# Attention scores from float32r parts on half of TensorE's rows, with maxima and exponentials of two heads side by side

## The reference

```python
q, k, v = proj(wq, bq), proj(wk, bk), proj(wv, bv)      # (4, 16, 1024, 16)
scores = jnp.einsum('bhqd,bhkd->bhqk', q, k) * scale
mask = jnp.triu(jnp.full((t, t), NEG, jnp.float32), k=1)
attn = jax.nn.softmax(scores + mask, axis=-1)
x = _layernorm(x + jnp.einsum('bhqk,bhkd->bhqd', attn, v).transpose(0, 2, 1, 3).reshape(b, t, d) @ wo + bo)
top1 = jnp.argmax(jnp.einsum('bh,he->be', x.mean(axis=1), Wr) + br, axis=-1)
x = _layernorm(x + relu(x @ W1[top1] + b1[top1]) @ W2[top1] + b2[top1])
```

## Time and profile before

| | us |
|---|---|
| median of 3 runs (956.9 to 964.15) | 957.01 |
| the profiled execution | 961.64 |
| its span, first to last instruction | 959.9 |
| PE busy in it | 803.6 (84%) |
| DVE busy | 636.3 (66%) |
| POOL busy | 452.2 (47%) |
| ACT busy | 441.7 (46%) |

### The profile page before, as it was taken

The page is one execution under the profiler, slowest core; times in us unless marked ns, Lnnn a source line. Parts: engine busy times, 40 slices in busy tenths (PEclk is TensorE's granted clock), DMA queues, the critical chain, the costliest instruction groups (busy, mean ns, idle before and its releaser), DMA issues.

```text
span 959.9 us, 16241 instructions
## 1 busy us (share of the span) xinstructions
PE 803.6 (84%) x5232; PEld 472.7 (49%) x5232; DVE 636.3 (66%) x2036; ACT 441.7 (46%) x801; POOL 452.2 (47%) x795
## 2 busy tenths in 40 slices
PE   3678879788988899979998799979998799992596
PEld 2333224224443455647672365647662365582586
DVE  1678768776888676756788677756888473262153
ACT  1005645554546565535445655535445557611231
POOL 6001324435354764544454764544454466664553
PEclk9769989999999999979999999979999799996799
DMA  3823531550525262302353262302343200002100
GB/s 102 102 27 39 101 43 14 101 68 3 68 63 80 66 111 38 44 13 30 50 88 76 57 111 40 41 13 32 49 48 78 85 12 14 13 12 65 40 23 23
DMA packets 44247, 49.99 MB, mean 52 GB/s; under 512 B 14722, under 2 KB 28802, under 8 KB 44162
## 3 DMA queue, kind: packets, MB, share of 16 engines
q1 hardware_dynamic: 44162, 48.95, 30.1%
HBM read 18.64 MB, written 4.19 MB: 24 GB/s over the span
## 4 chain that ended last, share of the span: by engine, by line
PE 58%; DVE 20%; SPq 6%; issue 5%; DMA 5%; POOL 3%; ACT 2%; DVEq 0%; POOLq 0%; ACTq 0%
PE o_ps L401 12%; PE max_ps L372 11%; PE dense_ps L495 9%; PE dense_ps L480 8%; PE exp_ps L385 8%; DVE max_ps L528 6%; PE dense_ps L419 5%; DVE partial_max L531 4%; PE dense_ps L430 3%; DMA stage<-in_w 2%; PE dense_ps L447 2%; DVE part_rest L565 2%; DMA inv_rows<-sums 1%; DVE partial_max L528 1%; DVE ln_in L639 1%
## 5 line engine op out<-in xcount | busy, mean ns | idle before, releaser
L718 ACT ACTIVATE prob<-exp_ps 128x512 f32<-128x512 f32 x576 | 333.1, 598 | 297.0 <-PE exp_ps L385 293.3
L528 DVE CUSTOM_DVE_ANT_0 max_ps<-max_ps,causal 128x512 f32<-128x512 f32 (+3 forms) x512 | 240.1, 512 | 96.5 <-PE max_ps L372 95.8
L372 PE MATMUL max_ps<-stack_k,stack_q 96*128 96x512 bf16 (+3 forms) x768 | 234.7, 349 | 72.2 <-DVE partial_max L528 31.7
L794 POOL TENSOR_SCALAR_AFFINE_SELECT prob<-prob 128x128 f32<-128x128 f32 x512 | 142.6, 299 | 252.3 <-ACT prob L718 250.9
L385 PE MATMUL exp_ps<-stack_q,stack_k 99*128 99x512 bf16 (+3 forms) x768 | 226.2, 337 | 18.9 <-ACT prob L718 15.5
L531 DVE TENSOR_REDUCE partial_max<-max_ps 128x1 f32<-128x512 f32 x256 | 171.3, 684 | 85.4 <-PE max_ps L372 84.8
L372 PEld LDWEIGHTS max_ps<-stack_k,stack_q 96*128 96x128 bf16 x768 | 67.1, 100 | 259.3 <-DVE partial_max L531 83.0
L401 PE MATMUL o_ps<-prob,v_ones 128*32 128x512 f32 (+3 forms) x1536 | 164.4, 517 | 0.0
L480 PE MATMUL dense_ps<-x1T_hi,w_hi 128*128 128x256 f32 x256 | 86.9, 339 | 35.0 <-POOL w_lo L844 21.4
L385 PEld LDWEIGHTS exp_ps<-stack_q,stack_k 99*128 99x128 bf16 x768 | 73.5, 100 | 65.1 <-ACT prob L718 27.1
L859 POOL TENSOR_TENSOR hidden_lo<-stage,hidden_hi 128x512 fp32r<-128x512 f32 x64 | 82.1, 1284 | 48.2 <-DVE hidden_hi L673 48.0
(11 more groups left out here) (73 smaller groups left out, 1016.6 us busy)
## 6 DMA issues: line engine op xcount, KB each, us to landing
stage<-in_w SPq DMA_DIRECT2D x32, 256.0 KB, 2.7
stack_k<-parts SPq DMA_DIRECT2D x64, 96.0 KB, 2.8
stack_q<-parts SPq DMA_DIRECT2D x64, 96.0 KB, 3.2
xT_sb<-in_xT SPq DMA_DIRECT2D x4, 1024.0 KB, 5.4
stack_k<-parts SPq DMA_DIRECT2D x64, 64.0 KB, 3.3
stack_q<-parts SPq DMA_DIRECT2D x64, 64.0 KB, 3.2
x<-in_x SPq DMA_DIRECT2D x4, 1024.0 KB, 6.7
out<-ln_in SPq DMA_DIRECT2D x16, 256.0 KB, 2.2
```

What stands on the lines that cost most here:

```text
L372: mm = TE.matmul(bank[:, at * P:(at + count) * P], stack_q[slot][0:ROWS, c, i * P:(i + 1) * P], stack_k[slot][0:ROWS, c, k0 * P:(k0 + coun ...
L528: op = VE.tensor_tensor_reduce(src, src, causal[:, BANK - count * P:], 1.0, MASKED, ALU.add, ALU.max, dst)
L718: SE.activation(prob[tile % P_RING][:, :], exp_ps[tile % 2][:, :], ACT.Exp, scale=scale).then_inc(s_exp, 1)
L794: GE.affine_select(out=part, in_=part, compare_op=ALU.is_ge, fill=0.0, base=0, pattern=[[1, P]], channel_multiplier=-1).then_inc(s_cut, 1)
```

## The change

Queries and keys are cut into two float32r parts rather than three bf16 ones. A head then needs 48 rows (50 with the maxima), which lie in one half of the array's 128 rows: heads 0 and 2 of a group in the lower, 1 and 3 in the upper. The order of the maxima tiles is such that in each step the maxima tile and the exponentials tile are of different halves. The causal constant is added to the maxima tile by TensorE: two more matmuls for each diagonal block, with a unit matrix, on the half of the tile's own head. So DVE needs one reduction for every tile. TensorE's program is written for two steps at a time: both steps' scores, then the products with the values, then the dense work. The inverses of the sums are spread by DMA rather than by DVE, each head's rows go to `attn` by DMA rather than by POOL's addition, v's bias is moved into bo by one product, and the sum of x1 is taken by TensorE (16 small products) rather than by POOL.

```diff
-PARTS = 3
+PARTS = 2
-ROWS3 = 3 * HD
-ROWS2 = ROWS3 + 2 * HD
-ROWS = ROWS2 + HD
+HALF = P // 2
+ROWS2 = 2 * HD
+ROWS = 3 * HD
...
+            def score(g, n, h, m):
+                c, u = max_of(n)
+                tile, slot, low = g * SLOTS + n, g % 3, HALF * (c % 2)
...
+                for s, (i, k0, count, at) in enumerate(MAX_UNITS[u]):
+                    diagonal = k0 + count == i + 1
+                    mm = TE.matmul(bank[:, at * P:(at + count) * P], q[:, i * P:(i + 1) * P],
+                                   k[:, k0 * P:(k0 + count) * P], start=True, stop=not diagonal)
+                    if s == 0 and h is not None:
+                        score_exp(h, m)
+                    for half in range(2 * diagonal):
+                        swapped = int(half != c % 2)
+                        mask = TE.matmul(bank[:, (at + count - 1) * P:(at + count) * P], unit_rows[rows, swapped, :],
+                                         causal[rows, swapped, :], start=False, stop=(half == 1))
...
-            for step in STEPS:
-                for g, n in plan.at("max", step):
-                    score_max(g, n)
-                for g, n in plan.at("exp", step):
-                    score_exp(g, n)
-                for n, piece in plan.at("dense", step):
-                    dense_piece(n, piece)
-                for g, u in plan.at("pv", step):
-                    values(g, u)
+            for two in range(0, plan.end, 2):
+                for step in (two, two + 1):
+                    maxima, exps = plan.at("max", step), plan.at("exp", step)
...
+                        score(g, n, h, m)
...
+                for step in (two, two + 1):
+                    for g, u in plan.at("pv", step):
+                        values(g, u)
+                for step in (two, two + 1):
+                    for n, piece in plan.at("dense", step):
+                        dense_piece(n, piece)
...
-                    if diagonal:
-                        op = VE.tensor_tensor_reduce(src, src, causal[:, BANK - count * P:], 1.0, MASKED, ALU.add,
-                                                     ALU.max, dst)
-                    else:
-                        op = VE.tensor_reduce(dst, src, AX_X, ALU.max)
+                VE.tensor_reduce(partial_max[:, g % 2, head_row(c), FIRST_CELL[u]:FIRST_CELL[u] + 4],
+                                 max_ps[tile % 2][:, :].rearrange("p (b k) -> p b k", b=4), AX_X,
+                                 ALU.max).then_inc(s_max_taken, 1)
...
+            def parts_lo(p, which, half):
...
+                VE.scalar_tensor_tensor(out=parts[:, which, 1, cols], in0=bank[:, :],
...
-                DMA.dma_start(k[0:ROWS3, c, :], src[:, 1, :, :]).then_inc(done, DMA_DONE)
...
+                DMA.dma_start(q[low:low + ROWS2, :], src[:, 0, :, :]).then_inc(done, DMA_DONE)
+                DMA.dma_start(k[low:low + ROWS2, :], src[:, 1, 0:1, :].broadcast_to([HD, 2, T])).then_inc(done, DMA_DONE)
+                DMA.dma_start(q[low + ROWS2:low + ROWS, :], src[:, 0, 0, :]).then_inc(done, DMA_DONE)
+                DMA.dma_start(k[low + ROWS2:low + ROWS, :], src[:, 1, 1, :]).then_inc(done, DMA_DONE)
...
+            def spread_inv(g):
+                sp.wait_ge(s_inv, DMA_DONE * (g + 1))
+                for c in range(G):
...
+            def send_o(g):
...
+                sp.wait_ge(s_scaled, HALVES * (g + 1))
...
+                for c in range(G):
+                    rows = slice(P // G * c + HD * (g % 2), P // G * c + HD * (g % 2) + HD)
+                    DMA.dma_start(attn[rows, r, :], o_sb[rows, :]).then_inc(s_attn, DMA_DONE)
...
+def max_of(n):
+    pair, place = n // (2 * UNITS), n % (2 * UNITS)
+    return 2 * pair + 1 - place % 2, place // 2
```

More of the change, by code:

```diff
@@ L43 @@
 V_NEEDED = [max(j for j, *_ in unit) // 2 for unit in EXP_UNITS]
[L46 to L54, removed]
+CELLS = 8
+CELL_ROWS = [2, 4, 1, 5, 0, 6, 3, 7]
+FIRST_CELL = [9, 26, 43, 56, 48, 60, 5, 39, 22]
 B, T, D, F, E = 4, 1024, 256, 1024, 8
@@ L169, in make_plan @@
             plan.put("v", unit, max(end + 1, clear) if b and t2 == 0 else end + 1)
+        elif kind == "bo":
+            plan.put("bo", unit, end + 1)
         elif kind == "rowturn":
@@ L433, in dense_piece @@
                         mm.then_inc(s_dense, 1)
+                elif kind == "bo":
+                    pe.wait_ge(s_load, LOADS)
+                    mm = TE.matmul(bank[:, 0:D], bv_sb[:, piece:piece + 1].broadcast_to([P, P]), wo_sb[:, piece, :],
+                                   start=(piece == 0), stop=(piece == PAIRS - 1))
+                    if piece == PAIRS - 1:
+                        mm.then_inc(s_dense, 1)
                 elif kind == "rowturn":
@@ L452, in dense_piece @@
                     b, = unit
-                    pe.wait_ge(s_add_up, ADDS * (b + 1))
                     for m in range(M):
-                        mm = TE.matmul(bank[:, m:m + 1], x1_sum[:, m * P:(m + 1) * P], ones[:, :], start=True, stop=True)
+                        for c in range(C):
+                            if m == 0 and c % 2 == 0:
+                                pe.wait_ge(s_ln_norm, plan.nth("ln_norm", ("wo", b, c // 2)))
+                            mm = TE.matmul(bank[:, m:m + 1], x1[b % 2][:, c, m * P:(m + 1) * P], ones[:, :],
+                                           start=(c == 0), stop=(c == C - 1))
                     mm.then_inc(s_dense, 1)
@@ L688, in _ @@
                     invert(g)
-                for unit in plan.at("spread", step):
-                    spread(*unit)
                 for ln in plan.at("ln_sum", step):
@@ L876, in _ @@
                     cut_future(g, n)
-                for unit in plan.at("parts", step):
-                    parts_low(*unit)
                 for ln in plan.at("ln_pow", step):
@@ L886, in _ @@
                     w_rest(*unit)
-                for unit in plan.at("add_up", step):
-                    add_up(*unit)
                 for unit in plan.at("b2", step):
@@ L998, in _ @@
                     send_inv(g)
+                for g, in plan.at("spread_inv", step):
+                    spread_inv(g)
+                for g, in plan.at("send_o", step):
+                    send_o(g)
                 for b, in plan.at("expert", step):
```

277 lines of the change are left out of this document (127 added, 150 removed).

## The result

The changed kernel takes 1093.2 us (median) against 960.6 for the kernel before: a ratio of 1.134, interval 1.123 to 1.145. The forecast was 889 and the range ended at 968. The profiled execution took 1092.6 us, with a span of 1090.9.

A forecast was written before the change was run, and what follows sets the result against it. TensorE's own work, and partly DVE's, was taken to bound the kernel. Terms of 55, 28, 2 and 10 us less, 21 and 5.6 more, gave 68 less: 961.6 to 893.2, forecast as an 889 us median, range 838 to 968.

The forecast's parts named there:

- the new wait: Rival, 6%: PE waits for ACT's exponentials in twos, 0.4 us for each of 144 products with the values, 58 us.
- PE's clock: In the batches, the granted clock was taken to stay at 0.95 to 0.97; a fall would refute the forecast.
- The lead: Opening stretch of maxima only: 48 us falls to 38 as DVE does less per tile; 10 us less (0 to 13).
- the end: After the last group, DMA spread, POOL's multiplications and further DMAs delay the output projection; 5.6 us more.
- The scores on PE: Score matmuls in the batches: overlapping halves cut a two-step pair from 0.88 to 0.68 us; 55 us less.
- Changes of shape: PE switching between full array, halves and column strips: 232 more changes at 0.09 us; 21 us more (0 to 46).
- DVE's waits: PE's 46 us of waiting for DVE's maxima: 60% goes because DVE has a fifth less work; 28 us less.
- Within the batches it costs nothing: The normalisation chain by DMA in the batches has six steps to spare before `wo`, so 0 us.
- Start: Before the first maxima tile: POOL's last part, a cast and buffer queueing go, more DMA issues come; 2 us less.

The follow-up runs named there:

- e8: e3 with DVE's maxima taken over only 32 of each 128 columns, leaving out three quarters of the scores; 998.9 us, ratio 1.041.
- e3: The changed kernel with DVE's, ACT's and POOL's programs also put in twos, like TensorE's; 1048.4 us, ratio 1.088.
- e13: The changed kernel with DVE spreading the inverses again and POOL writing the normalised rows straight to their place, without the DMAs; 1093.3 us, ratio 1.133.
- e14: e3 with the normalisation by DMA undone as in e13; 1030.2 us, ratio 1.068.
- e18: The kernel before with both kinds of score matmuls on the same 48 rows from row 0, leaving out part of the products; 1173.7 us, ratio 1.194.
- e17: e14 with maxima over only 32 of each 128 columns, as in e8; 946.1 us, ratio 0.988.
- e4: The changed kernel without the mask matmuls, so maxima are taken over future keys too; 1082.9 us, ratio 1.128.
- e11: The kernel before with only the change's normalisation: inverses spread by DMA and normalised rows sent to their place by DMA; 1051.0 us, ratio 1.095.
- e15: The kernel before with the causal mask by TensorE on the full array and one reduction per maxima tile, inverses still spread by DVE; 962.5 us, ratio 1.000.

## Why the prediction was wrong

The forecast failed at three steps: the 28 us that it took off PE's waits for DVE, the new wait that twos bring, which it left out of the sum as a rival at 6%, and PE's clock, which it held at its old level. The lead and the end were mis-sized as well. One by one:

- **The scores on PE: right, but for the masks.** The halves overlap, and the nearest row (column strips) was a good guide. The least-disturbed pairs cost 0.66, 0.83 and 1.03 us with no, four and eight masks, in 8, 4 and 6 of a group's 18 pairs: 0.82, of which 0.09 is the change of shape behind them. So 0.73 where 0.68 was said, 13 us over 266 pairs. A pair without masks costs the 0.57 that was said; the masks cost 0.16 rather than 0.11.
- **Changes of shape: right**, 0.09 us on both sides of a pair.
- **DVE's waits: this step failed.** I took 60% off 46 us because DVE had a fifth less to do; in the changed kernel they are 48. DVE's busy time did fall (548; 530 was said, 0.69 us per tile rather than 0.62). But a faster pair fills both banks and then stands until DVE has worked off the first, so a shorter PE stretch did not shorten the wait. That DVE's time per bank is what it waits for, e8 shows: lighter maxima took the wait from 41.8 to 6.0 us. Busy time cannot show this; the number of banks and the order of filling can.
- **The new wait, a rival at 6%: about its size, but too unlikely and in the wrong place.** It was to come at ACT behind the exponentials in twos, at 58 us. It came at dense work that ACT and DVE take by single steps and PE by twos: 45 us by e3, 63 with the normalisation undone too (e13 to e14).
- **PE's clock: the assumption that failed.** 0.95 to 0.97 was taken over from the rows of before and named as what would refute the forecast, but no case had a price for it. About 60 us are the clock, as an estimate. It could have been made a rival: scores went from 96 and 99 rows to 48 and 50. e18 shows what fewer rows do in the kernel before (0.52 in the first batch), and e8 and e17 that part of the loss goes when the stops go; how much of the 60 us belongs to which, no run divides.
- **The lead: failed.** 38 us were said, 59 measured. The forecast scaled DVE's time, which did fall (from 38 to 34 us). But PE's waits for DVE there are 9.2 us in both kernels; it is PE that is busy longer, 50 us instead of 38 at a clock of 0.71 and 0.72, with 10.5 us of masks that the lead's sum did not have. Masks alone are not it: without them (e4) the lead is 56.
- **The end: undersized.** 5.6 more were said, 14 measured, 12 to 13 of them the normalisation (e13, e14). The spread was costed at 3.6 us after the inverses and takes 8.9. Its landing time came from a small DMA.
- **"Within the batches it costs nothing": right here by luck.** In the kernel before the same part cost 91 us (e11), because POOL's queue stands behind it. I had looked for who waits for `attn`, not for what stands behind POOL's wait.
- **Start**: 2 us less were said; the first maxima start at 27.32 instead of 27.97.

The account from the changed kernel: 1093, less 45 for one order on all engines, less 18 for the normalisation, 1030; less 84 with three quarters of the maxima's work left out, and with it most of their wait and some of the clock's loss, 946. From there to the forecast 57 us stay, which no run divides.

No version that computes the whole reference beat the kernel before; e15 equals it.

## What to carry to other kernels

If work goes in twos, put it in twos on every engine that takes part: a queue that still goes by single steps makes the next tile wait for work that was moved behind it (45 us here, 38 in the kernel before). Before crediting a shorter burst with time, count the banks that it fills and ask how long the consumer needs for the first of them. And when matmuls go from most rows of the array to half of them, give the clock a case of its own.

## What the runs showed of the hardware

- Scores on 48 rows back to back, PE busy 98% of the stretch, ran at a granted clock of 0.52 (e18); the same columns on 96 to 99 rows, PE busy 83%, at 0.97. I had not expected rows to count at all.
- Taking work off PE can go with a lower clock and a longer stretch: without masks (e4) the first batch went from 0.81 to 0.68 and from 182 to 187 us in the one execution traced, though the whole kernel became 10 us shorter.
- Matmuls in the two row halves mostly start 3 to 4 ns apart when nothing waits (both at 405.31 above). The Trainium skill (TensorE: Matmul & The Clock Gate, Why this matters for your kernels) has matmuls in different row groups start within 4 ns; the trace agrees.
